# One layer-0 kernel: edge counts evicted by ScalarE, and the neighbour weights applied per tile in the memory stage

## The reference

```
h    = xn @ W_self.T + mean_over_in_edges(xn[src]) @ W_neigh.T + bias ; h = layernorm(h)*gamma + beta
mix  = mean(xn @ W_v.T) + xn @ ((xn @ W_theta.T).T @ (xn @ W_v.T)) / (n*sqrt(d))
x1   = x + h + mix
# memory: q = norm(x1) @ Wq; per head (8) two top-8 over 256 keys, top-8 of the 64 pairs -> 8 rows of a table
x2   = x1 + sum over heads, k of relu(norm(x1) . w_down[row]) * softmax(score) * w_up[row]
# layer 1 (attention over the same edges, another mix, an 8-expert feed-forward layer) follows
```

## Time and profile before

| what | us |
|---|---|
| median of three runs (2546.75 to 2559.88) | 2552.3 |
| the profiled execution | 2549.92 |
| its span on the core | 2548.4 |
| PE busy (87% of the span) | 2219.1 |
| DVE busy (54%) | 1388.4 |
| POOL busy (33%) | 837.8 |
| ACT busy (29%) | 750.1 |

### The profile page before, as it was taken

One profiled execution on the slowest core, in us unless ns is written; L12 is line 12 of the kernel. 1 busy time (PEld: TensorE's weight loads), 2 busy tenths in 40 slices (PEclk: granted clock), 3 DMA queues, 4 the chain that ended last, 5 costly groups with the idle time before them and its releaser, 6 DMA issues. The chain is left out here.

```text
span 2548.4 us, 32031 instructions
## 1 busy us (share of the span) xinstructions
PE 2219.1 (87%) x9444; PEld 1322.5 (52%) x9445; DVE 1388.4 (54%) x3843; ACT 750.1 (29%) x1737; POOL 837.8 (33%) x881
## 2 busy tenths in 40 slices
PE   8876889899899899999768898899999994999993
PEld 4333444444444444444314444799999541777771
DVE  4688338778778778779656112566666322000002
ACT  1012213323323323333222210466666210222220
POOL 0023227666676666667730000111110003111113
PEclk9988899999999999999898999899999995999996
DMA  4011139999999999999992033524422031322424
GB/s 137 10 42 76 79 133 382 358 373 344 363 375 341 364 371 345 368 374 371 261 240 101 1 114 104 152 80 124 125 78 78 26 121 44 125 103 103 166 101 133
DMA packets 152590, 483.29 MB, mean 190 GB/s; under 512 B 21908, under 2 KB 22580, under 8 KB 152368
## 3 DMA queue, kind: packets, MB, share of 16 engines
q0 software_dynamic: 99696, 354.10, 39.2%
q1 hardware_dynamic: 52800, 128.08, 15.4%
HBM read 445.44 MB, written 36.66 MB: 189 GB/s over the span
## 5 line engine op out<-in xcount | busy, mean ns | idle before, releaser
L536 POOL DMA_INDIRECT m_ring<-in_table,m_rows_at x640 | 644.7, 1007 | 332.0 <-PE m_acc L781 169.5
L781 PE MATMUL m_acc<-m_ring,m_diag 128*128 128x512 f32 x1280 | 614.6, 632 | 107.4 <-ACT m_diag L703 107.4
L781 PEld LDWEIGHTS m_acc<-m_ring,m_diag 128*128 128x128 f32 x1280 | 249.0, 200 | 443.5 <-issue 268.2
L596 DVE CUSTOM_DVE_ANT_0 m_ring<-m_ring,m_coming,m_part 128x512 f32<-128x512 f32 x640 | 442.1, 750 | 59.3 <-DMA m_ring<-in_table,m_rows_at 49.5
L703 ACT ACTIVATE m_diag<-ident,m_inner 128x128 f32<-128x128 f32 x640 | 219.6, 394 | 136.8 <-DVE m_inner L596 136.0
L1220 PE MATMUL a_psT<-v,a_pT 128*128 128x128 f32 x1600 | 199.7, 280 | 4.7 <-ACT a_pT L1310 0.5
L1220 PEld LDWEIGHTS a_psT<-v,a_pT 128*128 128x128 f32 x1600 | 184.6, 192 | 23.1 <-ACT a_pT L1310 23.0
L1764 PEld LDWEIGHTS e_psU<-e_rowsT,x_w 128*128 128x128 f32 x1472 | 170.4, 194 | 14.1 <-issue 14.1
L1764 PE MATMUL e_psU<-e_rowsT,x_w 128*128 128x128 f32 x1472 | 170.8, 278 | 2.8 <-DMA x_w<-in_we 1.7
L1773 PE MATMUL e_psY<-x_w,e_hT 128*128 128x512 f32 x368 | 161.7, 592 | 0.0
L680 ACT ACTIVATE m_qz<-m_psQ,m_bq 128x128 f32<-128x128 f32 x80 | 29.2, 366 | 448.4 <-PE m_psQ L757 448.4
(11 more groups left out here) (301 smaller groups left out, 2747.6 us busy)
## 6 DMA issues: line engine op xcount, KB each, us to landing
x_w<-in_we SPq DMA_DIRECT2D x16, 2048.0 KB, 11.5
a_mask<-edge_masks SPq DMA_DIRECT2D x40, 320.0 KB, 2.9
a_cnt<-edge_counts SPq DMA_DIRECT2D x40, 320.0 KB, 2.9
m_ring<-in_table,m_rows_at POOLq DMA_INDIRECT x640, 6.3
qk_parts<-p_parts SPq DMA_DIRECT2D x32, 320.0 KB, 4.2
a_k<-qk_parts SPq DMA_DIRECT2D x32, 320.0 KB, 7.6
edge_shares<-shareT SPq DMA_DIRECT2D x10, 640.0 KB, 2.9
m_share<-edge_shares SPq DMA_DIRECT2D x10, 640.0 KB, 7.2
```

Source lines behind the costliest of these rows:

```text
L536: pool.indirect_dma_start(ring[0:n, slot, :], None, ins["table"], bass.IndirectOffsetOnAxis(rows_at[0:n, h, k:k + 1], 0)).then_inc(s_land[ ...
L596: dve.tensor_tensor_reduce(ring[:, slot, 0:D], ring[:, slot, 0:D], coming[:, t % 2, :], part[:, b, k:k + 1], 0.0, ALU.mult, ALU.add, inner ...
L781: pe.matmul(acc[:, :], diag[:, h % 2 * TOPK + k, :], ring[:, nth % RING, D:2 * D], start=h + k == 0, stop=h * TOPK + k == HEADS * TOPK - 1 ...
```

## The change

Five edits come together:

1. The Gram matrix is symmetric; only its upper blocks are computed (512, 384, 256 and 128 columns in place of four times 512), and the lower ones come from 6 transposes. The normed rows of all tiles are kept in `xn_rows`, which takes the place of `neigh`; DVE no longer waits for PE between tiles.
2. The mean term and DVE's addition to all rows stand in the middle of the kv chains, not after counting.
3. Counting: POOL has no part in it. ACT writes 16-bit counts straight from PSUM and then the mask (as +1e30 where there is no edge, so the sign of the queries, the minimum and the exponent in the attention is turned). The one-hot buffers are doubled: four for even and four for odd tiles.
4. The 40 products xn @ W_neigh are gone. In the memory stage the share of a tile is multiplied with `xn_rows` first (`gather_near`, 40 products of 128 columns into `psT`), ACT copies the result to `aggT`, and 4 products of 512 columns with W_neigh finish the layer. The six pieces are now: kv, gather, gather, W_self, W_neigh (2 products), W_neigh (2 products).
5. `LAST_ROWS` is gone: the last tile fetches 128 rows per DMA, too.

The core of the diff:

```diff
-            with pool.Fori(0, NT // 2) as j:
-                for b in range(2):
-                    t = j * 2 + b
-                    pool.wait_ge(s["cnt_out"], t + 1)
-                    wait_alone(c, pool, s["stored"], t * 32)
-                    pool.tensor_copy(cnt16[:, :], cnt[:, b, :]).then_inc(s["cnt16"], 1)
-
-                    pool.tensor_scalar(mask[:, :], cnt[:, b, :], 0.0, NEG, ALU.is_equal, ALU.mult).then_inc(s["cnt16"], 1)
+            pool.memset(unlinked[:, :], -NEG).then_inc(s["unlinked"], 1)
...
+                    mm = pe.matmul(psB[:, m, m * P:D], xn[:, t, m * P:(m + 1) * P], xn[:, t, m * P:D], start=t == 0,
+                                   stop=t == NT - 1, skip_group_check=True)
...
-                    act.wait_ge(s["cnt16"], t * 2 - 2)
                     act.wait_ge(s["share"], t - 1)
-                act.activation(cnt[:, b, :], C2[b][:, 0:NP], ACT.Copy, accum_out=deg[:, b:b + 1]).then_inc(s["cnt_out"], 1)
+                    act.wait_ge(s[f"stored{b}"], t * 16 - b * 16)
+                act.activation(cnt16[:, b, :], C2[b][:, 0:NP], ACT.Copy, accum_out=deg[:, b:b + 1]).then_inc(s["cnt_out"], 1)
+                act.activation(mask[:, b, :], C2[b][:, 0:NP], ACT.Relu, bias=unlinked[:, :], scale=NEG).then_inc(s["masked"], 1)
...
-            for t in range(NT):
-                if t >= 2:
-                    pe.wait_ge(s["nout"], t - 1)
-                for k in range(KC):
-                    mm = pe.matmul(psB[:, t % 2, :], c.xnT[:, k, t * P:(t + 1) * P], wn[:, k, :], start=k == 0, stop=k == KC - 1)
-                mm.then_inc(s["near"], 1)
...
-                n = P if t < NT - 1 else LAST_ROWS
...
-                        pool.indirect_dma_start(ring[0:n, slot, :], None, ins["table"],
-                                                bass.IndirectOffsetOnAxis(rows_at[0:n, h, k:k + 1], 0)).then_inc(s_land[slot], 16)
+                        pool.indirect_dma_start(ring[:, slot, :], None, ins["table"],
+                                                bass.IndirectOffsetOnAxis(rows_at[:, h, k:k + 1], 0)).then_inc(s_land[slot], 16)
...
+        def gather_near(pe, u, lo, hi):
+
+            if lo == 0:
+                pe.wait_ge(s["share_in"], u * 16 + 16)
+            for k in range(lo, hi):
+                for a in range(NT):
+                    mm = pe.matmul(psT[:, k * P:(k + 1) * P], xn[:, a, k * P:(k + 1) * P], share[:, a, :], start=a == 0, stop=a == NT - 1)
+            if hi == KC:
+                mm.then_inc(s["near"], 1)
+
+        def layer(pe, u, piece):
+
+            tile = slice(u * P, (u + 1) * P)
+            if piece == 0:
+                if u:
+                    pe.wait_ge(s["x1"], u)
+                for k in range(KC):
+                    pe.matmul(psH[:, 0, :], c.xnT[:, k, tile], kv[:, k, :], start=k == 0, stop=k == KC - 1)
+            elif piece < 3:
+                gather_near(pe, u, 2 * piece - 2, 2 * piece)
+            elif piece == 3:
+                for k in range(KC):
+                    pe.matmul(psH[:, 1, :], c.xnT[:, k, tile], ws[:, k, :], start=k == 0, stop=False)
+            else:
+                if piece == 4:
+                    pe.wait_ge(s["nearT"], u + 1)
+                for k in range(2 * piece - 8, 2 * piece - 6):
+                    mm = pe.matmul(psH[:, 1, :], aggT[:, k, :], wn[:, k, :], start=False, stop=k == KC - 1)
+                if piece == 5:
+                    mm.then_inc(s["layer"], 1)
 
         def project(pe, q, b):
...
                 if j and t + 2 < NT:
-                    layer(pe, t + 2, (j - 1) * 6, (j - 1) * 6 + 3)
+                    layer(pe, t + 2, 2 * j - 2)
```

More of the change, by code:

```diff
@@ L133, in stage_prepare @@
     nc, ins = c.nc, c.ins
-    neigh, kv = keep
-    ws, keys, bias, gamma = ahead
+    xn, kv = keep
+    ws, wn, keys, bias, gamma = ahead
     with ExitStack() as st:
@@ L383, in _ @@
             pe.wait_ge(s["edges"], 2)
-            pe.sem_inc(s["gram"], 1)
-            def tile(t, b, first):
+            for t in range(NT):
                 pe.wait_ge(s["rows"], t + 1)
-                if not first:
+                if t >= 2:
                     pe.wait_ge(s["tdone"], t - 1)
                 for k in range(KC):
-                    mm = pe.transpose(psT[:, b, k * P:(k + 1) * P], rows[:, b, k * P:(k + 1) * P], c.ident[:, :])
+                    mm = pe.transpose(psT[:, t % 2, k * P:(k + 1) * P], xn[:, t, k * P:(k + 1) * P], c.ident[:, :])
@@ L392, in tile @@
                 mm.then_inc(s["tr"], 1)
                 for m in range(KC):
-                    mm = pe.matmul(psB[:, m, :], rows[:, b, m * P:(m + 1) * P], rows[:, b, :], start=first and b == 0,
-                                   stop=True, skip_group_check=True)
-                mm.then_inc(s["gram"], 1)
-            for b in range(2):
-                tile(b, b, True)
-            with pe.Fori(1, NT // 2) as j:
-                for b in range(2):
-                    tile(j * 2 + b, b, False)
@@ L403, in _ @@
-            pe.wait_ge(s["w"], 64)
-            pe.matmul(psB[:, 4, 0:P], c.ident[:, :], c.ident[:, :], start=True, stop=True).then_inc(s["gdone"], 1)
-            for m in range(2 * KC):
-                left, right = (gram, wv) if m < KC else (wth, m1)
-                if m < KC:
-                    pe.wait_ge(s["gout"], KC)
-                if m >= 2:
-                    pe.wait_ge(s["ev"], m - 1)
-                if m == KC:
+                    mm = pe.matmul(psB[:, m, m * P:D], xn[:, t, m * P:(m + 1) * P], xn[:, t, m * P:D], start=t == 0,
+                                   stop=t == NT - 1, skip_group_check=True)
@@ new lines, in _ @@
+            mm.then_inc(s["gram"], NT)
+            pe.wait_ge(s["w"], 48)
+            pe.wait_ge(s["tdone"], NT)
+            pe.wait_ge(s["gout"], KC)
+            for n in (3, 2, 1):
+                for m in range(n):
+                    mm = pe.transpose(FLIP[n][:, m * P:(m + 1) * P], gram[:, m, n * P:(n + 1) * P], c.ident[:, :])
+                mm.then_inc(s["flip"], 1)
+            for i in range(2 * KC):
+                left, right, m = (gram, wv, KC - 1 - i) if i < KC else (wth, m1, i - KC)
+                if i == 1:
+                    pe.wait_ge(s["flipped"], 3)
+                if i >= 2:
+                    pe.wait_ge(s["ev"], i - 1)
+                if i == KC:
+                    pe.wait_ge(s["bar"], 1)
+                    for k in range(KC):
+                        mm = pe.matmul(psT[:, 1, :], xbar[:, k, :], wv[:, k, :], start=k == 0, stop=k == KC - 1)
+                    mm.then_inc(s["sum"], 1)
@@ L412, in _ @@
                     pe.wait_ge(s["ev"], KC)
                 for k in range(KC):
-                    mm = pe.matmul(psB[:, 4 + m % 2, :], left[:, k, m % KC * P:(m % KC + 1) * P], right[:, k, :],
+                    mm = pe.matmul(psB[:, 4 + i % 2, :], left[:, k, m * P:(m + 1) * P], right[:, k, :],
                                    start=k == 0, stop=k == KC - 1)
                 mm.then_inc(s["mm"], 1)
-            pe.wait_ge(s["ev"], 2 * KC)
-            pe.wait_ge(s["tdone"], NT)
             pe.wait_ge(s["zero"], 1)
-            pe.sem_inc(s["hot_free"], 4)
+            for b in range(2):
+                pe.sem_inc(s[f"hot_free{b}"], 4)
@@ L421, in _ @@
             pe.wait_ge(s["bounds"], 1)
-            done = pe.alloc_register("groups_done")
-            pe.reg_mov(done, 0)
+            pe.wait_ge(s["mean"], 1)
+            done = [pe.alloc_register(f"groups_done{b}") for b in range(2)]
+            for b in range(2):
+                pe.reg_mov(done[b], 0)
             def count(t, b):
                 many = pe.value_load(bounds[0:1, bass.ds(t + NT, 1)], min_val=1, max_val=NG // 2)
-                before = pe.snap(done)
+                before = pe.snap(done[b])
@@ L785, in _ @@
         def _(pe):
-            layer(pe, 0, 0, PRODUCTS)
+            for piece in range(PIECES):
+                layer(pe, 0, piece)
             pe.wait_ge(s["w"], 32)
@@ L795, in _ @@
                     project(pe, q + 1, b)
-            layer(pe, 1, 0, PRODUCTS)
+            for piece in range(PIECES):
+                layer(pe, 1, piece)
             for q in range(last_pair + 1):
```

193 lines of the change are left out of this document (93 added, 100 removed).

## The result

The changed kernel takes 2476.1 us (median of 4 runs, 2468.6 to 2482.9), the kernel before on the same chip 2549.5: ratio 0.9715, 95% interval 0.9687 to 0.9743. The forecast was 2486.

| from mark to mark | before | after | difference | foretold |
|---|---|---|---|---|
| start to first matmul of counting | 85.67 | 73.77 | -11.9 | -11 |
| to ScalarE's last copy of counts | 189.35 | 155.15 | -34.2 | -34 |
| to the first DMA of the memory stage | 54.80 | 18.65 | -36.2 | -35 |
| to the turning of the rows of tile 1 | 74.44 | 85.44 | +11.0 | +9 |
| to that of tile 9 | 758.43 | 788.16 | +29.7 | +30 |

A forecast was written before the change was run, and what follows sets the result against it. Counting was taken as bound by DVE, itself stalled by POOL, the memory loop by PE's program, the last tile by DMA. Terms -11 - 34 - 35 + 9 + 30 - 23 = -64 took 2549.9 to 2486 us, range 2457 to 2525.

The forecast's parts named there:

- Gram matrix: Before counting: fewer Gram columns, mean term moved in, no wait for the last copy of kv; -11 us.
- end of the stage: From last count to memory stage: neighbour products, mean term and their copies go; 20.1 us in place of 55.1, -35.
- Counting: Counting stage: POOL's stalls go and each tile costs about the clean tile; 155 us in place of 188.6, -34.
- The 114 for the hots: Counting stage: 184 hots at DVE's pace of 0.62 us each.
- 32 + 4: Counting stage: 32 us for transposes, waits and ACT's mask in 8 tiles, some 4 for start and first two tiles.
- The cross-check: Counting stage: nine stalls of 4.3 us removed, ten masks on ACT added, giving 162 us.
- Tiles 0 and 1: Start of memory stage: layer longer by 3.8 us in both tiles, plus 1.5 waiting for the share; +9.
- Memory loop: Eight memory tiles: 3.8 us more layer work each, paid in full on PE; +30, period 95.4 to 99.2.
- The rival in which the gaps take the layer: Memory loop: PE's waits at tile start absorb the added 3.8 us, kernel 2456 us; chance 0.07.
- Last tile: Last memory tile: 128 rows in place of 112, slots at 1.35 us in place of 1.70; -23.
- by bytes: Last memory tile: pace per byte stays, slots at 1.94 us, tile 124 us, kernel 2524; chance 0.14.
- equal rows: Last memory tile: identical padding rows served one by one, slot 3.64 us, tile 233, kernel 2633; chance 0.04.

The follow-up runs named there:

- the last experiment: Changed kernel with ScalarE's copies of the turned shares first and the neighbour products back in counting, partly between the last turnings: 2445.7 us, 0.9577 of the kernel before.
- the ladder: Changed kernel fetching 128, 128, 128, 120, 112, 104, 96, 64, 128 and 128 rows per DMA in the ten memory tiles: 2544.2 us, one run.
- the second group: Runs on one slower chip: neighbour products moved back, turned shares copied first, layer pieces in PE's gaps; kernel before 2651.4 us, changed kernel 2587.8.
- that of the first: Chip of the first group: 112 rows again, GpSimd masks, single hot buffers, neighbour products moved back; kernel before 2637.4 us, unaltered changed kernel not run.

## Why the prediction was right, term by term

*Gram matrix* (-11.9 for -11) and *end of the stage* (-36.2 for -35) came as worked out; the memory stage begins at 247.6 us where 249 stood.

*Counting* was right in its sum (-34.2 for -34) and in its cause, which the run with GpSimd's masks shows: 38.4 us for that edit alone. The sum splits otherwise than foretold. The 114 for the hots are 116.1 of busy matmuls, but not as 184 times VectorE's 0.62: a hot costs PE's 0.57 where the clock is full and up to 0.7 where it is not, so what the clock costs lies in here. The rest, put at 32 + 4, is 39: each tile has 4.7 to 5.3 beside its hots where 4.0 stood. That the parts add up to 155 almost exactly is in part luck. The prediction had the mask "exposed on PE in each of the 8 tiles", which was right (PE's wait for ScalarE went from at most 1.2 to 2.4 us, in all from 6.6 to 16.6), and took it as the price of the edit, which it was not: it was a matter of ScalarE's order, and the run with the copies first gives 15 back. What I gave to the doubled hot buffers, nothing, is what they are worth. The cross-check counted nine stalls of 4.3, one per tile but for one; the trace of before has seven, and five of about 1.0 behind casts, 35 us in place of 38.

*Tiles 0 and 1* (+11.0 for +9): the wait for the share that I put at 1.5 is not there. It landed 5.0 us after its issue, and PE reached the gather only after 5.95 us, because the eight matmuls with kv ahead of it took 6.12 in place of 3.6, behind the stretch at a granted clock of 0.58 shown above:

```profile
247.62 6.12 PE L748 MATMUL m_psH<-kv,xnT 128*128 128x512 f32 x8 [4.90 <-PEq L77]
253.57 9.09 PE L737 MATMUL m_psT<-m_share,xn_rows 128*128 128x128 f32 x80
```

The sum for these tiles was nearly right for the wrong reason; and the layer of the second tile cost 4.8 in place of 3.8.

*Memory loop* (+29.7 for +30): the period went from 95.42 to 99.0, with the gaps where they were. That work added between the gaps is paid in full is borne out by the last experiment: taking the 3.6 us out of the layer brings back 95.42. The rival in which the gaps take the layer is out.

*Last tile* (-29.9 for -23): the mechanism was right and its size too small. The prediction took 1.35 us per slot, "as the mean includes PE's waits", and it is 1.28 in the rows shown, 1.24 on average: by VectorE's timeline the last tile's slots take 78.0 us from first to last in place of 106.6, and 1.3 more lie in the tile before, into which the first fetches of the last one reach. This is most of the 10 us by which the forecast was too high. Its reason, that fewer rows came with a slower pace, is now shown: 26 us in a run that undoes this edit alone, and the step at 128 partitions in the ladder. The rivals by bytes and by equal rows are out.

*The rest* (-2.2 for 0) is within what two runs differ.

So of the two halves in the change's name, one carries the gain. Counting without GpSimd gives 34 to 38 us. Multiplying in the memory stage costs 40.7 there (11.0 + 29.7) and saves 36.2 at the end of the stage of counting (33.4 by the runs that undo it): by the stages a loss of 4 to 8 us, hidden in the sum by the 128 rows and the shorter Gram matrix.

## What to carry to other kernels

Look at the row count of indirect DMAs: here, with rows of 4 KB, a slot of 112 useful rows is faster with 16 rows of padding fetched beside them, and every count below 128 that was tried had the slow pace. When an engine is taken out of a path, look at the order in which its successor does the work: here ScalarE's mask stood ahead of copies that PE waits for. When one wait is removed, ask who sets the pace next: here it was VectorE, which took what the clock would have given. Moving dense PE work between two stages that are both PE's gains only what it can hide beside. It gained between the last turnings, where PE waited for work that did not hang on it; in the two gaps of the memory loop it only moved the gaps.

## What the runs showed of the hardware that was not expected

*The step at 128 partitions.* Per busy time of the DMA engines, 367 to 390 GB/s at 128 rows and 238 to 263 at 120, 112, 104, 96 and 64.

*A cast stalls VectorE, too.* Five one-hots of 0.25 us took 1.24 to 1.29 in the kernel before, each while GpSimd cast the counts; the seven of 4.5 us stood beside its masks.

*Two chips with a slower memory loop.* On the chip of the second group the changed kernel's tile takes 106 to 112 us in place of 99, and its kin on that of the first are as slow, though packets are as short (159 ns) and the DMA engines' share is 0.85 in place of 0.95. ScalarE holds PE up there:

```profile
873.04 0.37 ACT L669 ACTIVATE m_qz<-m_psQ,m_bq 128x128 f32<-128x128 f32 x1 [14.18 <-remote]
```
```profile
867.25 0.70 PE L778 MATMUL m_psS<-keys,m_qz 64*128 64x256 f32 x4
873.46 1.23 PE L778 MATMUL m_psS<-keys,m_qz 64*128 64x256 f32 x4 [5.50 <-ACT m_qz L669]
```

The products that this ACTIVATE reads ended at 865.6 (PE, 864.55 + 1.05), 7.4 us earlier; on the faster chip the same instruction starts at 802.02, where they end at 801.98. Nothing in the trace shows what releases it so late. The wait comes once per tile with the same 7.4 us, and another of about 6 us in the same tile; together they are somewhat more than the 11 us by which the tile is longer. The trace's loads of instructions do not explain it: an 8 KB load starts at 855.3, 17.7 us ahead, and of the 12 such waits from 360 to 1100 us, 8 have no load in the 12 us before they end. The cause is open. It is why the kernels of those groups are judged by their stages and by their neighbours, and why the loop's gain in the second group is hidden in its noise.
